# Three more waits ahead of the gathers in the attention walks of a graph network with experts

## The chip, the cores and the metric

The kernel runs on one core of a Trainium2 chip. The metric is the device time of one execution in microseconds (us), as the median of several runs; lower is better. TensorE's clock has two levels, 1.2 and 2.4 GHz; a granted clock of 1.00 in the profile is all of a stretch at the upper one.

## The reference

Four layers, each a graph attention followed by a mixture of experts, over 3125 nodes with 256 features and 50000 edges sorted by destination. What matters here is the attention of layers 0 and 1 and the two attentions of layer 2, which all have this form:

```python
h = jnp.einsum('nd,dhf->nhf', x, W)
al_s = jnp.sum(h * a_src, axis=-1)
al_d = jnp.sum(h * a_dst, axis=-1)
logits = jax.nn.leaky_relu(al_s[src] + al_d[dst], NEG_SLOPE)
m = jax.ops.segment_max(logits, dst, num_segments=num_nodes)
e = jnp.exp(logits - m[dst])
z = jax.ops.segment_sum(e, dst, num_segments=num_nodes)
alpha = e / (z[dst] + 1e-16)
msg = h[src] * alpha[..., None]
out = jax.ops.segment_sum(msg, dst, num_segments=num_nodes)
```

Layer 3's attention also needs a product of the 256 attributes of every edge with a matrix. Its terms are computed in pieces inside the four walks below.

## The kernel before, in words

The function `gat_edges` (from L708) walks over the edges once. It runs four times: for layer 0 and layer 1 (names `l_edges_...`, called from `gat_layer`) and twice for layer 2 (`l2a_edges_...` and `l2b_edges_...`, called from `gat_pair`). The edges are laid out in 416 tiles of 128; 16 tiles are a chunk (CK = 16), so a walk has NCK = 26 chunks. A chunk is worked on in four groups of 4 tiles (GR = 4, NG4 = 4).

Every engine has its own program, written by hand, and they meet by semaphores:

- GpSimd (POOL) issues one gather for each tile (L774): 128 rows of `h_rows`, picked by the tile's source nodes, come from HBM into `stage`. `stage` has SL = 3 slots, one chunk in each. The gathers of group g of chunk c wait until the messages of group g of chunk c - 3 are made (`msg_built`), for then that part of the slot is free. The first three chunks wait for nothing. The order is plain: chunk by chunk, group by group.
- VectorE, in chunk c, makes the messages of a group (`weigh`, L893), rescales the accumulator (L901), makes the logits of chunk c + 1 (`logits`, L828, L831, L833; L831 is the reader of `stage` that waits for the gathers of chunk c + 1), and then takes a step of the running maximum of chunk c + 1 in each group: `tile_ends` (two scans, L838 and L840, and L844), `tile_tops` (scans L853 and L855, L858, L860) and `edge_maxima` (L869, scans L872 and L877, L875). Behind them stand `exponents` (L886, L887) and `nodes_hot` of chunk c + 2 (L823, a transposed one-hot of 2048 columns). In between it adds the finished sums of the group before to the accumulator (L912).
- TensorE (PE), in chunk c, adds up messages by destination (`scatter`, L1081), a group at a time. After group 0 it transposes the logits of chunk c + 1 (L1053, `lg_turned`), after group 1 it places the tile ends (L1057, `ends_placed`), after group 2 the carried maxima (L1062, `inits_made`), in the middle of group 3 it places the rescaling (L1071) and turns the maxima of the edges (L1067, `max_turned`). Around these stand the transposes and products of the edge attributes (L1032, L1039) and the expansion of the destinations' terms of chunk c + 2 (L1047).
- ScalarE (ACT) makes the one-hot matrices for the scatter (L959, L962), the exponentials (L971, L975), and copies the attributes' products out of PSUM (L979, L985).
- SyncE (SP) loads `rel_b` and the edge attributes `ea` and stores the products `e_s` to `e_rows`; it waits for `hotT_built`, `ea_turned` and `e_kept`.

The steps that meet the change, in the words of the code (VectorE, then TensorE):

```python
dve.wait_ge(ends_placed, c + 1)      # tile_tops, before L853
dve.wait_ge(inits_made, c + 1)       # edge_maxima, before L869
dve.wait_ge(max_turned, c + 1)       # exponents, before L886 / L887
...
scatter(c, 1); place_ends(c + 1); attr_terms(c, 0)
scatter(c, 2); place_tops(c + 1); turn_attr(c, m, 1, None)
scatter(c, 3, 0, GR // 2); place_f(c + 1); turn_maxima(c + 1)
```

Of the kernel before, what the change touches and what calls it, by code (L numbers as in the profile page):

```python
# [707 lines left out]
def gat_edges(nc, K, name, h_rows, adp, acc, loops, part):  # L708
# [5 lines left out]
    SL, PER = 3, 6  # L714
    assert (NCK - 2) % PER == 0 and PER % SL == 0 and PER % 2 == 0
    with Phase(nc, name) as ph:
# [49 lines left out]
        with nc.Block() as block:  # L766
            @block.gpsimd
            def _(pool):
                for c in range(NCK):
                    for g in range(NG4):  # L770
                        if c >= SL:
                            pool.wait_ge(msg_built, NG4 * (c - SL) + g + 1)
                        for u in range(g * GR, (g + 1) * GR):
                            nc.gpsimd.indirect_dma_start(out=stage[:, c % SL, u, :], out_offset=None, in_=h_rows,  # L774
                                                         in_offset=bass.IndirectOffsetOnAxis(ap=K.src_t[:, c * CK + u:c * CK + u + 1], axis=0)).then_inc(gathered[c % SL], 16)
# [2477 lines left out]
```

## Time and profile before

| | us |
|---|---|
| median of 3 runs | 7633.64 |
| lowest and highest of them | 7617.78, 7638.52 |
| span of the profiled execution | 7653.2 |
| PE busy | 4967.7 (65%) |
| VectorE busy | 3878.6 (51%) |
| ScalarE busy | 2369.9 (31%) |
| GpSimd busy | 2994.7 (39%) |
| gathers L774 in the four walks | 1664 |

The profiled execution's own time is its span, 7653.2 us, 0.26% above the median of the runs. Busy time of an engine counts its instructions that compute, and for GpSimd the issuing of gathers. Over a program with many stages the shares are averages; what a stage is worth is read in the stretch where it runs.

### The profile page before, as it was taken

What the parts mean: (1) busy time and instruction counts of PE and PEld (TensorE: products, weight loads), DVE (VectorE), ACT (ScalarE), POOL (GpSimd) and SP (SyncE); (2) the same over time, 40 slices, a digit from 0 to 9 for tenths busy, and PEclk for the clock granted to TensorE, in tenths of its full rate; (3) what the DMA queues carried; (4) which work ended last, traced back from release to release, by engine and by line L of the source; (5) the groups of instructions that cost most, each with busy time, mean ns of one, the idle gap of its engine ahead of it and who ended that gap; (6) DMA issues with size and microseconds to landing.
All of it is one profiled execution on the core that took longest, in us unless ns stands there. A gap on an engine that the chain in (4) does not pass through costs nothing. (4 is left out here: it accounts for less than half of the span.)

```text
span 7653.2 us, 80105 instructions
## 1 busy us (share of the span) xinstructions
PE 4967.7 (65%) x19379; PEld 3450.2 (45%) x19380; DVE 3878.6 (51%) x8350; ACT 2369.9 (31%) x5733; POOL 2994.7 (39%) x2942
## 2 busy tenths in 40 slices
PE   1466657726666746666366564777799755557999
PEld 1344435524444534444244443444377533346676
DVE  4355562345556335555355565666611587777211
ACT  0233322213333223333133332444422122245333
POOL 1554423344453034443444434555400277633000
PEclk9677768857777877778677776888899866678899
DMA  4444413334443023333343331111100499954000
GB/s 111 126 129 122 120 40 117 99 97 118 119 123 91 13 78 118 117 120 99 109 122 118 117 101 26 28 26 28 16 17 13 174 374 366 337 155 148 9 12 21
DMA packets 563283, 817.74 MB, mean 107 GB/s; under 512 B 108537, under 2 KB 441942, under 8 KB 562790
## 3 DMA queue, kind: packets, MB, share of 16 engines
q0 software_dynamic: 141088, 377.21, 17.8%
q1 hardware_dynamic: 397914, 425.15, 17.2%
q10 hardware_dynamic: 23952, 11.93, 0.6%
q8 instruction: 93, 1.52, 0.1%
q14 instruction: 236, 1.93, 0.1%
HBM read 656.93 MB, written 157.49 MB: 106 GB/s over the span
## 5 line engine op out<-in xcount | busy, mean ns | idle before, releaser
L774 POOL DMA_INDIRECT l_edges_stage<-l_h_rows,src_t x832 | 801.9, 964 | 861.4 <-DVE l_edges_msg L893 524.2
L1081 PE MATMUL l_edges_ps_sum<-l_edges_msg,l_edges_hot 128*128 128x264 f32 x1664 | 611.2, 512 | 350.7 <-DVE l_attn_acc L912 154.6
L2511 POOL DMA_INDIRECT l_edge_kv<-l_kv_rows,src_t x416 | 471.3, 1133 | 695.7 <-POOLq L2419 547.8
L2933 POOL DMA_INDIRECT l_gate_edges_srow<-l_gate_src_rows,l_gate_edges_idx x512 | 488.7, 954 | 399.5 <-DVE l_gate_edges_val L2990 187.3
L1081 PEld LDWEIGHTS l_edges_ps_sum<-l_edges_msg,l_edges_hot 128*128 128x128 f32 x1664 | 364.4, 244 | 520.4 <-issue 252.1
L3069 PE MATMUL l_gate_edges_ps<-l_gate_edges_wide,l_gate_edges_hot_lo 128*128 128x500 f32 x1024 | 510.0, 657 | 122.5 <-ACT l_gate_edges_hot_lo L3026 94.3
L774 POOL DMA_INDIRECT l2a_edges_stage<-l2a_h_rows,src_t x416 | 399.9, 961 | 450.0 <-DVE l2a_edges_msg L893 280.1
L774 POOL DMA_INDIRECT l2b_edges_stage<-l2b_h_rows,src_t x416 | 399.9, 961 | 433.6 <-DVE l2b_edges_msg L893 269.2
L2564 PE MATMUL l_edge_ps_q<-l_q_q,l_edge_hot 128*128 x832 | 340.7, 581 | 309.4 <-issue 231.8
L1081 PE MATMUL l2b_edges_ps_sum<-l2b_edges_msg,l2b_edges_hot 128*128 128x272 f32 x832 | 318.7, 530 | 181.1 <-issue 80.0
L2564 PEld LDWEIGHTS l_edge_ps_q<-l_q_q,l_edge_hot 128*128 128x128 f32 x832 | 232.7, 293 | 417.5 <-issue 371.5
L1081 PE MATMUL l2a_edges_ps_sum<-l2a_edges_msg,l2a_edges_hot 128*128 128x272 f32 x832 | 308.9, 516 | 154.7 <-issue 86.6
L912 DVE TENSOR_TENSOR l_attn_acc<-l_attn_acc,l_edges_ps_sum 128x264 f32 x832 | 350.2, 421 | 82.4 <-DVE l_attn_acc L912 32.7
L3069 PEld LDWEIGHTS l_gate_edges_ps<-l_gate_edges_wide,l_gate_edges_hot_lo 128*128 128x128 f32 x1024 | 215.9, 217 | 377.2 <-issue 232.7
L2692 DVE SCALAR_TENSOR_TENSOR x<-l_experts_psb,l3f_g,x 128x256 f32<-128x256 f32 x200 | 96.8, 484 | 434.1 <-PE l_experts_psb L2723 434.1
L1081 PEld LDWEIGHTS l2b_edges_ps_sum<-l2b_edges_msg,l2b_edges_hot 128*128 128x128 f32 x832 | 186.7, 250 | 273.1 <-issue 137.3
L2995 DVE TENSOR_TENSOR l_gate_edges_wide<-l_gate_edges_hot_hi,l_gate_edges_val 128x500 f32<-128x500 f32 x512 | 305.5, 669 | 2.2
L2761 ACT ACTIVATE l_experts_hT<-l_experts_psa,l_experts_sc_pair 128x320 f32<-128x320 f32 x320 | 195.3, 611 | 355.1 <-PE l_experts_psa L2714 334.6
L3024 ACT ACTIVATE l_gate_edges_hot_lo<-col,l_gate_edges_nlo 128x128 f32<-128x128 f32 x512 | 156.5, 388 | 436.3 <-DMA l_route_b<-in_L_ffn_gate_b 214.8
L1081 PEld LDWEIGHTS l2a_edges_ps_sum<-l2a_edges_msg,l2a_edges_hot 128*128 128x128 f32 x832 | 181.5, 243 | 242.1 <-issue 146.6
L893 DVE TENSOR_TENSOR l_edges_msg<-l_edges_stage,l_edges_ps_p 128x1056 f32<-128x1056 f32 x208 | 259.5, 1248 | 21.0 <-issue 20.8
L985 ACT COPY l_edges_e_s<-l_edges_ps_e 128x512 f32<-128x512 f32 x96 | 56.3, 586 | 687.7 <-DMA sched_kx<-ends 226.6
(799 smaller groups left out, 11098.5 us busy)
## 6 DMA issues: line engine op xcount, KB each, us to landing
l_edge_e<-e_rows SPq DMA_DIRECT2D x416, 128.0 KB
l_val_rows<-l_edge_vj SPq DMA_DIRECT2D x104, 512.0 KB
l_agg_stage<-l_val_rows SPq DMA_DIRECT2D x52, 1024.0 KB, 5.6
l_edges_rel_b<-rel_rows SPq DMA_DIRECT2D x52, 512.0 KB
l_edges_ea<-in_edge_attr SPq DMA_DIRECT2D x48, 512.0 KB
e_rows<-l_edges_e_s SPq DMA_DIRECT2D x48, 512.0 KB, 5.3
l_experts_w<-in_L_ffn_w SPq DMA_DIRECT2D x32, 512.0 KB, 5.1
l_gate_edges_lo_b<-l_gate_edges_lo_rows SPq DMA_DIRECT2D x64, 256.0 KB
```

The lines of the kernel that those rows point to most:

```text
L774: nc.gpsimd.indirect_dma_start(out=stage[:, c % SL, u, :], out_offset=None, in_=h_rows, in_offset=bass.IndirectOffsetOnAxis(ap=K.src_t[:, ...
L893: nc.vector.tensor_tensor(msg[:, g % 2, :, 0:HW].rearrange("p u (h c) -> p u h c", c=HC), stage[:, i % SL, g * GR:(g + 1) * GR, 0:HW].rear ...
L912: nc.vector.tensor_tensor(to, to, ps_sum[u][:], ALU.add).then_inc(added, 1)
L1081: nc.tensor.matmul(ps_sum[u][:], hot[:, g, u, :], msg[:, g % 2, u, :], start=True, stop=True).then_inc(summed, 1)
L2511: nc.gpsimd.indirect_dma_start(out=kv[:, m, u, :], out_offset=None, in_=kv_rows, in_offset=bass.IndirectOffsetOnAxis(ap=K.src_t[:, n * EB ...
L2564: last = nc.tensor.matmul(ps_q[2 * s + u // 2][:, u % 2, :], hot[:, s, u * P:(u + 1) * P], q[:, bass.ds(ids[n % 4 * EB + u], 1), :].rearra ...
L2692: nc.vector.scalar_tensor_tensor(acc[:, tile, :], psb[(v * GT + t) % 2][:], gates[:, tile, bass.ds(j * 2 + v // NG, 1)], acc[:, tile, :], ...
L2761: nc.scalar.activation(hT[l][:, v % 2, f, half * HALF:half * HALF + cols], psa[n % NA][:, 0:cols], ACT.Relu, bias=sc_pair[:, 1, l, v // NG ...
L2933: nc.gpsimd.indirect_dma_start(out=srow[:, n % 4, u, :], out_offset=None, in_=src_rows, in_offset=bass.IndirectOffsetOnAxis(ap=idx[:, n * ...
L2995: nc.vector.tensor_tensor(wide[:, s, u], bcast(hot_hi[:, n % 3, u, :], GV), val[s][:, u, :].unsqueeze(1).to_broadcast([P, NT, GV]), ALU.mu ...
L3024: nc.scalar.activation(hot_lo[:, s, u, :], K.col[:], ACT.Abs, bias=nlo[:, n * GB + u:n * GB + u + 1]).then_inc(near_lo, 1)
L3069: nc.tensor.matmul(flat, hot_lo[:, n % 2, u, :], wide[:, n % 2, u].rearrange("p t f -> p (t f)"), start=False, stop=False).then_inc(summed, 1)
```

## The change

When gathers of chunk c have to wait at all (c >= 3), group 1 now also waits until TensorE has placed the tile ends of chunk c - 2, group 2 until it has placed the carried maxima of chunk c - 2, and group 3 until it has turned the maxima of chunk c - 2. Group 0 is as before. The program of no other engine is altered.

```diff
                     for g in range(NG4):
                         if c >= SL:
                             pool.wait_ge(msg_built, NG4 * (c - SL) + g + 1)
+                            if g == 1:
+                                pool.wait_ge(ends_placed, c - SL + 2)
+                            elif g == 2:
+                                pool.wait_ge(inits_made, c - SL + 2)
+                            elif g == 3:
+                                pool.wait_ge(max_turned, c - SL + 2)
                         for u in range(g * GR, (g + 1) * GR):
```

## Rows read from the trace of the kernel before

**Rows 1.** The page of the profiled execution, first line.
```profile
span 7653.2 us, 80105 instructions
```

**Rows 2.** Stretches: us; PE, PEld, VectorE, ScalarE, POOL busy (count); clock; DMA share; GB/s.
```profile
300.60:981.20 680.60, 428.78 (x1805) 294.32 (x1802) 360.76 (x838) 226.75 (x572) 339.21 (x352) 0.78 0.42 122
1737.70:2424.40 686.70, 433.04 (x1819) 295.69 (x1815) 361.17 (x838) 227.10 (x573) 339.16 (x352) 0.77 0.43 121
2891.20:3592.50 701.30, 438.89 (x1809) 297.30 (x1806) 367.57 (x860) 238.39 (x661) 338.39 (x352) 0.77 0.41 119
3820.80:4523.00 702.20, 437.71 (x1822) 298.10 (x1821) 367.19 (x859) 238.71 (x661) 338.01 (x352) 0.77 0.42 119
3592.50:3628.60 36.10, 27.27 (x138) 17.05 (x134) 32.23 (x78) 22.00 (x63) 0.00 (x0) 1.00 0.09 30
```

**Rows 3.** Waits of VectorE over the span: us in total, times, longest.
```profile
DVE l_edges_init L869 <- remote: 266.4, 32, 11.6
DVE l2a_edges_init L869 <- DMA l_experts_xs<-pair_rows: 164.3, 20, 11.2
DVE l2b_edges_init L869 <- DMA l_edges_stage<-l_h_rows,src_t: 150.1, 19, 9.1
```

**Rows 4.** A chunk of walk l2a in time: start, us, engine, line [idle before <-releaser].
```profile
3105.62 0.16 DVE L869 COPY l2a_edges_init<-l2a_edges_ps_w 128x2 f32<-128x2 f32 x1 [8.35 <-DMA l_experts_xs<-pair_rows]
...
3110.03 0.29 DVE L886 TENSOR_TENSOR l2a_edges_last_max<-l2a_edges_ps_w,last_t 128x128 f32<-128x128 f32 x1 [1.55 <-PE l2a_edges_ps_w L1067]
...
3114.91 0.96 POOL L774 DMA_INDIRECT l2a_edges_stage<-l2a_h_rows,src_t  x1 [12.09 <-DVE l2a_edges_msg L893]
...
3120.52 0.23 PE L1057 MATMUL l2a_edges_ps_w<-l2a_edges_placed,of_head 128*8 128x32 f32 x2
...
3125.69 0.27 DVE L853 TENSOR_TENSOR_SCAN l2a_edges_run<-links_f,l2a_edges_top,l2a_edges_ps_w 8x32 f32<-8x32 f32 x1 [4.72 <-DMA out_rows<-l_experts_y]
...
3130.80 0.93 PE L1062 MATMUL l2a_edges_ps_w<-ones,l2a_edges_spread 8*128 8x1 f32 x4
...
3134.00 0.96 POOL L774 DMA_INDIRECT l2a_edges_stage<-l2a_h_rows,src_t  x1 [0.30 <-issue]
3137.64 0.59 ACT L985 COPY l2a_edges_e_s<-l2a_edges_ps_e 128x512 f32<-128x512 f32 x1 [12.57 <-DMA pair_rows<-l0f_acc,l0f_slot]
3137.79 0.16 DVE L869 COPY l2a_edges_init<-l2a_edges_ps_w 128x2 f32<-128x2 f32 x1 [7.66 <-DMA l_experts_xs<-pair_rows]
```

**Rows 5.** Another chunk of the same walk in order of time.
```profile
2986.78 0.95 POOL L774 DMA_INDIRECT l2a_edges_stage<-l2a_h_rows,src_t  x1 [3.61 <-DVE l2a_edges_msg L893]
...
2991.03 0.27 PE L1053 MATMUL l2a_edges_ps_w<-ident,l2a_edges_lg 128*128 128x128 f32 x1
...
2995.46 0.42 DVE L838 TENSOR_TENSOR_SCAN l2a_edges_local<-cuts_f,l2a_edges_ps_w 128x128 f32<-128x128 f32 x1 [3.52 <-DMA l_experts_w<-in_L_ffn_w]
...
3000.19 0.28 PE L1057 MATMUL l2a_edges_ps_w<-l2a_edges_placed,of_head 128*8 128x32 f32 x2
...
3000.61 0.27 DVE L853 TENSOR_TENSOR_SCAN l2a_edges_run<-links_f,l2a_edges_top,l2a_edges_ps_w 8x32 f32<-8x32 f32 x1 [1.42 <-PE l2a_edges_ps_w L1057]
...
3005.83 0.16 DVE L869 COPY l2a_edges_init<-l2a_edges_ps_w 128x2 f32<-128x2 f32 x1 [0.77 <-PE l2a_edges_ps_w L1062]
...
3008.28 0.33 PE L1067 MATMUL l2a_edges_ps_w<-ident,l2a_edges_seg_max 128*128 128x128 f32 x1
...
3008.91 0.95 POOL L774 DMA_INDIRECT l2a_edges_stage<-l2a_h_rows,src_t  x1 [0.30 <-issue]
...
3011.05 0.29 DVE L886 TENSOR_TENSOR l2a_edges_last_max<-l2a_edges_ps_w,last_t 128x128 f32<-128x128 f32 x1 [2.36 <-DMA l0f_gb<-in_L_ffn_beta]
...
3015.93 0.95 POOL L774 DMA_INDIRECT l2a_edges_stage<-l2a_h_rows,src_t  x1 [6.07 <-DVE l2a_edges_msg L893]
```

**Rows 6.** Line L774: durations in ns, and who waited for it.
```profile
L774 POOL DMA_INDIRECT l2b_edges_stage<-l2b_h_rows,src_t x416: 948/957/1374, 3722.2 to 4511.8; - x139
...
  DVE l_edges_z L831: 4.4, 2
```

## The prediction, made before the changed kernel was run

> **What bounds the kernel now.** I read the page first, then the stretches of the four attention walks, then the waits, then two single chunks in order of time. The profiled execution spans 7653.2 us [rows 1]. Each walk has 26 chunks. In chunks 1 to 22 the gathers of chunks 4 to 25 are issued beside the arithmetic, and the four stretches that hold them are 680.6, 686.7, 701.3 and 702.2 us long, 352 gathers in each [rows 2]. That is 2770.8 us for 88 chunks, 31.5 us a chunk, 36% of the span. Two chunks at the end of a walk, when no gather is left, take 36.1 us together, so 18.1 us each, with the same arithmetic and the clock granted at 1.00 in place of 0.77 [rows 2]. No engine is full: in the third stretch PE is busy 438.9 of 701.3 us, POOL 338.4 [rows 2]. So a chunk loses 13.4 us to something that the gathers bring.
>
> What it is shows where VectorE waits. Its copy of the carried maxima (L869) alone waits 266.4, 164.3 and 150.1 us [rows 3], 580.8 us in all, and the releasers named there ("remote", a DMA of another phase, the gathers) are not what L869 waits for: in the code it waits for inits_made, which TensorE raises at L1062. In one chunk in order of time [rows 4], the first of 16 gathers starts at 3114.91 and the last at 3134.00, 1.27 us apart. The tile ends (L1057) start on PE at 3120.52 and take 0.2 us, yet VectorE's scan behind them starts at 3125.69. The carried maxima (L1062) start at 3130.80 and take 0.93 us; VectorE's copy starts at 3137.79, 6 us after they end, and ScalarE, idle 12.6 us for a signal of PE, starts at 3137.64. Both start 3.6 us after the last gather started. My reading is that TensorE's signals are held back while a long burst of gathers is under way, and let go together when it has ended. I see no other limit in this stage.
>
> **What the change does, step by step.** Per walk, for chunks 3 to 25 (23 of them), POOL gets three more waits, 276 in all; no instruction that computes and no DMA is added or removed. Group 0 of chunk c still follows the messages of chunk c-3. Group 1 now also waits for ends_placed of chunk c-2, group 2 for inits_made, group 3 for max_turned: each is a signal that TensorE raises about one quarter of a chunk later than the message that released the group so far. So one burst of 16 becomes four bursts, each cut off until the signal that VectorE wants next has got through. Call the starts of the four bursts T0 to T3.
>
> *T0 to T1.* With 4 gathers behind a clear pause, the ends' matmul ends 5.8 us after the first gather (3114.91 to 3120.72 [rows 4]); that is the low end. The other chunk [rows 5] has four bursts of 4 already, by chance: there T0 is 2986.78, and the turned logits, ready on PE at 2991.30, reach the scan L838 at 2995.46, because group 1 had followed group 0 at once and kept the hold up. The last gather of group 0 starts at 2990.7 (2986.78 and three steps of 1.3), and behind the last gather of group 3 the hold is let go after 2.1 us (3008.91 to 3011.05), so 2992.9 would have been possible, 2.5 us sooner. The ends are done at 3000.47, 13.7 us after T0, less 2.5 is 11.2; the high end. I take 10.0, near the high end, since group 3 of the chunk before will stand right ahead of group 0, as a burst of 8, and the logits will be held much as in rows 5.
>
> *T1 to T2.* From the scan L853 at 3000.61 to the copy L869 at 3005.83: 5.2 us, with gathers running [rows 5]. Above it a full hold: 3.8 us to the last of four gathers and 3.6 us more as in rows 4, 7.4. I take 5.6.
>
> *T2 to T3.* 3005.83 to 3011.05 is 5.2 us with gathers, L1067 ending at 3008.61 and held until 2.1 us after the gather at 3008.91 [rows 5]; without gathers 4.4 (3105.62 to 3110.03 [rows 4]); above, 7.4 again. I take 5.2.
>
> *T3 to the next T0.* 4.9 us in either chunk (3110.03 to 3114.91 [rows 4], 3011.05 to 3015.93 [rows 5]). POOL itself needs four times 1.27, 5.1, before it can start group 0, so this part becomes POOL's. Group 3 now also meets VectorE's building of the transposed one-hot (L823, after L887), which few gathers do today. Rows bound that: a gather takes 957 ns in the middle and 1374 at most [rows 6], so between nothing and 0.4 us. I take 5.4. The Trainium skill, SBUF — State Buffer, section "Who interferes with whom", says that a tensor_scalar in a two-port mode holds GpSimd off the shared port until it is done; by that rule alone the loss could be the whole length of L823; no gather of this trace was lengthened by more than 0.4 us.
>
> Sum: 10.0 + 5.6 + 5.2 + 5.4 = 26.2; I add 0.5 for chunks that are longer than the pattern for reasons I can't place, 26.7. The ends give 5.8 + 5.2 + 4.4 + 5.1 = 20.5 and 11.2 + 3 x 7.4 = 33.4. Present pattern as a check: 3105.62 to 3137.79 is 32.2 us [rows 4]. The gain is 31.5 - 26.7 = 4.8 us a chunk, 88 times, 422 us. I cost nothing for chunk 0 of each walk, where 48 gathers run ahead without a wait, and for the last three chunks, which have none. I cost nothing for the later landing of the gathers: group 3 goes off at most a chunk later and is wanted two chunks on by L831, which today waited on gathers 4.4 us in the first two walks together [rows 6]; if that cover went, L831 would wait and every chunk with it. Behind POOL's new waits stand only further gathers; SP's queue and the phase's end wait for none of them. 7653.2 - 422 = 7231 for the profiled execution; the median of the runs, 7633.64, lies 20 us under its span, so 7211, and I say 7210.
>
> **The rivals.** *Signals pass freely* (13%). If a burst of 4 holds nothing, and 8 in a row little, a chunk is 20.5 to 24.5 us, gain 7 to 11 us, 616 to 968 in all: 6665 to 7020. For: the copy L869 waited 0.77 us there, against 7.66 in rows 4 [rows 5]. Against: L1067 in the same rows, ready at 3008.61 and seen at 3011.05.
>
> *The spacing takes most of it back* (17%). The chunk of rows 5 was split in four by chance and still took 29.2 us (3015.93 - 2986.78). If only the last tenths change there, 29 to 31.2 us: 7415 to 7610.
>
> *Slower* (12%). If a burst of 4 is already long enough to hold every signal for the full 3.6 us behind its last gather, each stage is 7.4 us, and stage T0 has a second round trip in it, as logits and ends follow each other (2995.46 to 3000.19, 4.7 us [rows 5]): 4 x 7.4 + 4.7 = 34.3, 2.8 us a chunk over today, 247 us: up to 7880. POOL would idle while PE's signals wait, and the overlap of gathers with the stage behind would be lost. It decides from a mean hold that brings the sum over 31.5. Against it stand the 2.1 us behind the last gather and the short wait of L869 in rows 5.
>
> *No change* (6%). The hold may have nothing to do with the bursts' length: 7634. The Trainium skill, SBUF — State Buffer, section "Who interferes with whom", has it that a DMA never contends with a compute engine and that PE and ACT wait for nobody; by that rule the gathers could not cost TensorE's readers anything. Rows 2 (18.1 us against 31.5) speak against it, though the clock differs as well and might be cause rather than effect: were PE at 0.77 the cause, the chunk's idle would be PE's busy time and not waits of 6 us.
>
> **How the numbers follow.** The forecast, 24.5 to 29 us a chunk, 7020 to 7415, has 52%. A measurement of this kernel can tell about 0.3%, 23 us. Faster by more: 52 + 13 + 17 = 82%; within 6%; slower 12%. Range: up to 7640, which takes in no change and leaves the slower case out, and down to 6900, leaving some 5% below.
>
> **What would show it.** Right: POOL's gathers (L774) wait for PE's L1057, L1062 and L1067; bursts of 4, 4 and 8; L869's wait falls from 580.8 us to under 150; the four stretches shrink to about 590 us each; granted clock there above 0.77. T0 wrong: L838 waits about as long as L853 does today, or not at all. Wrong as a whole: L853, L869 and L886 each wait 2 us or more after PE has ended, in every chunk, and the distance of L893's first groups stays at 31 us or grows.

## The result, and the profile after

The changed kernel takes 7437.02 us as the median of 4 runs (7404.3 to 7447.07), the kernel before, beside it, 7636.08 us (7617.78 to 7644.19): a ratio of 0.974, with a 95% interval of 0.9711 to 0.977. The profiled execution spans 7445.3 us, 208 less than before [rows 1].

The four stretches of chunks 1 to 22, cut by the same instructions as before [rows 2], with the same columns:

```profile
299.50:955.10 655.60, 460.62 (x1805) 318.51 (x1805) 362.50 (x837) 227.39 (x573) 338.85 (x352) 0.79 0.42 127
1710.40:2361.40 651.00, 448.61 (x1806) 311.50 (x1805) 362.68 (x837) 228.37 (x574) 337.37 (x352) 0.80 0.43 128
2826.20:3442.40 616.20, 445.78 (x1804) 298.12 (x1804) 367.10 (x860) 239.48 (x657) 342.97 (x352) 0.81 0.46 135
3669.10:4292.80 623.70, 447.94 (x1805) 301.81 (x1804) 367.40 (x860) 240.79 (x660) 341.09 (x351) 0.80 0.45 133
```

They sum to 2546.5 us against 2770.8: 224.3 us less, 28.94 us a chunk against 31.49. The start of each walk, from its first gather to the first message of chunk 1, is 2.3 to 3.8 us shorter, 13.3 us in all; its end, from the first message of chunk 23 on, is 0.9 to 3.6 us longer, 7.7 us in all. The rest of the program gives about 22 us back, most of it behind the last message of the last walk, 3099.9 us against 3081.1. The kernels below, with the same program there and on chips where the kernel before takes about 7640 us, have 3067.6 to 3109.9 us in that place, so I read this as scatter.

The waits of POOL and of VectorE over the span (us in total, times, longest). The line numbers are 6 higher than before: L844 is the first reader of the turned logits, L859 of the tile ends, L875 of the carried maxima (L869 of [rows 3]), L893 of the turned maxima, L834 of the expansion of the destinations' terms.

```profile
POOL l_edges_stage L780 <- PE l_edges_ps_w L1063: 331.7, 41, 15.0
DVE l_edges_x L893 <- remote: 205.0, 45, 7.3
DVE l_edges_ad L834 <- remote: 170.8, 39, 23.3
DVE l_edges_local L844 <- remote: 104.5, 30, 5.0
DVE l_edges_init L875 <- remote: 22.5, 4, 9.9
DVE l_edges_init L875 <- PE l_edges_ps_w L1068: 21.5, 38, 1.3
```

The wait for the carried maxima, 580.8 us by the rows shown before [rows 3] and 613.0 us with the smaller ones of the same line, is 102 us now with all of them (44.0 here for layers 0 and 1). In its place stand waits for the turned maxima (L893), the turned logits (L844) and the expansion (L834). One chunk of layer 0, in order of time:

```profile
565.10 1.04 POOL L780 DMA_INDIRECT l_edges_stage<-l_h_rows,src_t  x1 [2.56 <-remote]
...
570.22 0.97 POOL L780 DMA_INDIRECT l_edges_stage<-l_h_rows,src_t  x1 [0.31 <-issue]
...
572.70 0.42 PE L1059 MATMUL l_edges_ps_w<-ident,l_edges_lg 128*128 128x128 f32 x1
...
574.03 0.97 POOL L780 DMA_INDIRECT l_edges_stage<-l_h_rows,src_t  x1 [0.30 <-issue]
...
576.76 0.42 DVE L844 TENSOR_TENSOR_SCAN l_edges_local<-cuts_f,l_edges_ps_w 128x128 f32<-128x128 f32 x1 [4.90 <-remote]
...
581.37 0.28 PE L1063 MATMUL l_edges_ps_w<-l_edges_placed,of_head 128*8 128x32 f32 x2
...
582.43 0.95 POOL L780 DMA_INDIRECT l_edges_stage<-l_h_rows,src_t  x1 [7.43 <-PE l_edges_ps_w L1063]
...
585.55 0.60 PE L1068 MATMUL l_edges_ps_w<-ones,l_edges_spread 8*128 8x1 f32 x4
...
586.19 0.16 DVE L875 COPY l_edges_init<-l_edges_ps_w 128x2 f32<-128x2 f32 x1
...
587.47 0.96 POOL L780 DMA_INDIRECT l_edges_stage<-l_h_rows,src_t  x1 [0.30 <-issue]
...
588.61 0.33 PE L1073 MATMUL l_edges_ps_w<-ident,l_edges_seg_max 128*128 128x128 f32 x1
...
591.25 0.96 POOL L780 DMA_INDIRECT l_edges_stage<-l_h_rows,src_t  x1 [0.30 <-issue]
...
594.01 0.29 DVE L893 TENSOR_TENSOR l_edges_x<-l_edges_lg,l_edges_ps_w 128x128 f32<-128x128 f32 x1 [5.00 <-remote]
...
594.76 1.04 POOL L780 DMA_INDIRECT l_edges_stage<-l_h_rows,src_t  x1 [2.55 <-remote]
```

The gathers go in two bursts of eight. The first is group 3 of one chunk (from 565.10) and group 0 of the next (from 570.22, T0), the second is group 1 (582.43, T1) and group 2 (587.47, T2). Group 2 starts 5.04 us after group 1, four gathers' pitch: its new wait ends before POOL gets there. A signal raised early in a burst passes: the carried maxima, placed at 585.55 with 0.60 us of matmuls, are read at 586.19, 3.8 us into the burst. A signal raised later does not: the turned logits are done at 573.12 and read at 576.76, 2.7 us after the last gather of the burst has started (574.03); the turned maxima are done at 588.94 and read at 594.01, 2.8 us after the last gather (591.25). So the chunk is 12.2 + 5.0 + 7.3 + 5.1 = 29.6 us.

It isn't the reader that is slow. The trace also records the semaphores' updates: that of the turned logits at 576.62, 3.5 us after their matmul's end and 0.14 before the scan, that of the turned maxima at 593.99, 5.05 us after theirs and 0.02 before L893. The one of the tile ends, outside a burst, comes 0.01 us after its matmul (581.65, 581.66). As the profile models the ends of matmuls, this doesn't say whether in a burst the matmul itself or only its update is late.

The means from the starts of the gathers' groups, chunks 4 to 25 of each walk, whose gathers go beside chunks 1 to 22 (worked out from all rows of L780, us):

| | T0 to T1 | T1 to T2 | T2 to T3 | T3 to T0 | a chunk, 1 to 22 |
|---|---|---|---|---|---|
| layer 0 | 12.28 | 5.25 | 6.88 | 5.40 | 29.80 |
| layer 1 | 11.80 | 5.08 | 7.19 | 5.53 | 29.59 |
| layer 2, first | 10.42 | 5.52 | 6.45 | 5.62 | 28.01 |
| layer 2, second | 10.94 | 5.51 | 6.43 | 5.55 | 28.35 |
| all | 11.36 | 5.34 | 6.74 | 5.53 | 28.94 |

Chunk 3, the first whose gathers wait, is left out: its T0 to T1 is 18.6 to 20.6 us.

In layer 2 chunks of 24 to 26 us and of 31 to 36 us alternate over parts of the walks: T0 to T1 is about 7.8 us in the short ones and 13.7 to 16.7 in the long ones, 14 of the 44. One of the long ones, in order of time:

```profile
3089.77 0.95 POOL L780 DMA_INDIRECT l2a_edges_stage<-l2a_h_rows,src_t  x1 [1.79 <-DMA l_experts_xs<-pair_rows]
...
3092.86 0.29 DVE L892 TENSOR_TENSOR l2a_edges_last_max<-l2a_edges_ps_w,last_t 128x128 f32<-128x128 f32 x1 [0.97 <-PE l2a_edges_ps_w L1073]
...
3103.94 0.95 POOL L780 DMA_INDIRECT l2a_edges_stage<-l2a_h_rows,src_t  x1 [0.30 <-issue]
...
3107.08 0.56 DVE L834 TENSOR_REDUCE l2a_edges_ad<-l2a_edges_ps_ad 128x128 f32<-128x384 f32 x1 [9.22 <-remote]
...
3115.15 0.95 POOL L780 DMA_INDIRECT l2a_edges_stage<-l2a_h_rows,src_t  x1 [10.26 <-PE l2a_edges_ps_w L1063]
```

Here group 2's wait did last (1.79 us idle before 3089.77). The turned maxima then passed, 3.1 us into the burst (3092.86), and groups 3 and 0 followed with no pause: a burst of 12, up to 3103.94. It held the expansion until 3107.08, 3.1 us after its last gather, the logits stand behind that, and T1 is 3115.15, 15 us after T0 (3100.17).

### The profile page after: what moved, and what is told of

Read it like the earlier page. It is cut to its first block and busy times, and to the rows that moved or that the text cites. A ratio compares the mean times of both kernels' runs of the same rounds, so it can differ in the third digit from the quotient of the medians.

```text
span 7445.3 us, 80381 instructions
## 1 busy us (share of the span) xinstructions
PE 5031.1 (68%) x19379; PEld 3497.1 (47%) x19380; DVE 3881.1 (52%) x8350; ACT 2376.9 (32%) x5733; POOL 3003.7 (40%) x2942
## 5 line engine op out<-in xcount | busy, mean ns | idle before, releaser
L780 POOL DMA_INDIRECT l_edges_stage<-l_h_rows,src_t x832 | 799.6, 961 | 806.6 <-PE l_edges_ps_w L1063 331.7
L780 POOL DMA_INDIRECT l2a_edges_stage<-l2a_h_rows,src_t x416 | 404.7, 973 | 361.8 <-issue 111.7
L780 POOL DMA_INDIRECT l2b_edges_stage<-l2b_h_rows,src_t x416 | 403.8, 971 | 362.3 <-issue 113.3
L1045 PE MATMUL l_edges_ps_e<-l_edges_we,l_edges_eaT 128*128 128x256 f32 x768 | 238.9, 464 | 86.0 <-issue 73.5
```

The costliest lines, as they stand in the source:

```text
L1045: last = nc.tensor.matmul(ps_e[0:n, u * D:(u + 1) * D], eaT[:, u, k, 0:n], we[:, k, :], start=(k == 0), stop=(k == DC - 1))
```

## The experiments

The first kernels take single waits of the change away.

**One wait, on the ends.** Edit against the changed kernel:

```diff
                             if g == 1:
                                 pool.wait_ge(ends_placed, c - SL + 2)
-                            elif g == 2:
-                                pool.wait_ge(inits_made, c - SL + 2)
-                            elif g == 3:
-                                pool.wait_ge(max_turned, c - SL + 2)
```

> Of the three new waits only the one of group 1 (ends_placed) is kept. Theory (TensorE's signals are held while gathers follow one another and are let go 2.6 us after the last one has started; the first 4 us of a burst let them pass): groups 1 to 3 go as one burst of 12 from T1, the turned maxima come free at T1 + 13.9 + 2.6 = 16.5, group 0 starts 4.6 later, alone behind a pause, so that ends_placed is there 6 to 7.8 us after it. 27.1 to 28.9 us a chunk, against 28.9 with all three waits: 7360 to 7440 us. Rival (each wait brings its share of the gain): a third of the 199 us of the change, about 7570.

Measured: 7358.04 us against 7644.86 of the kernel before beside it, 0.963 (0.9614 to 0.9646), 28.20 us a chunk. One chunk in order of time:

```profile
445.91 0.96 POOL L776 DMA_INDIRECT l_edges_stage<-l_h_rows,src_t  x1 [3.60 <-DVE l_edges_msg L895]
...
459.37 0.29 DVE L889 TENSOR_TENSOR l_edges_x<-l_edges_lg,l_edges_ps_w 128x128 f32<-128x128 f32 x1 [6.77 <-remote]
459.81 1.34 POOL L776 DMA_INDIRECT l_edges_stage<-l_h_rows,src_t  x1 [0.30 <-issue]
465.54 0.95 POOL L776 DMA_INDIRECT l_edges_stage<-l_h_rows,src_t  x1 [4.39 <-DVE l_edges_msg L895]
```

Groups 1 to 3 are a burst of 12 (445.91 to 459.81), which holds the turned maxima for 6.8 us and lets them go 0.4 us before its last gather starts, not after it; group 0 then stands alone, since its messages are late, and T0 to T1 is 8.5 us, the last stage 8.9 to 9.5 in most chunks. One wait alone brings at least as much as the three. The chunk lies where it was expected, but by parts that make up for each other: the turned maxima are free 13.5 us after T1 in place of 16.5, group 0 starts 6.2 us later in place of 4.6, and T0 to T1 takes 8.5 in place of 6 to 7.8.

**Without the wait of group 2, and with that of group 3 alone.**

```diff
-                            elif g == 2:
-                                pool.wait_ge(inits_made, c - SL + 2)
```

```diff
-                            if g == 1:
-                                pool.wait_ge(ends_placed, c - SL + 2)
-                            elif g == 2:
-                                pool.wait_ge(inits_made, c - SL + 2)
-                            elif g == 3:
+                            if g == 3:
                                 pool.wait_ge(max_turned, c - SL + 2)
```

> The wait of group 2 (inits_made) is left out, those of groups 1 and 3 stay. Theory: group 2 starts 5.0 us after group 1 in most chunks of the changed kernel, which is POOL's own pace, so this wait decides nothing: within 25 us of the changed kernel's 7437. Rival (the three waits together make four bursts): loses a part of the gain, 7500 or more.

> Of the three new waits only the one of group 3 (max_turned) is kept. Theory: groups 3, 0 and 1 go as a burst of 12, the turned logits of the next chunk are held until 16.5 us after it began, then ends, carried maxima and turned maxima follow, each 4 to 6 us later: about 31 us a chunk, as without any wait, 7560 to 7680 us. Rival (each wait brings its share): about 7570; rival (it is the wait ahead of the loads that matters, since gathers no longer meet them): near the changed kernel, 7440.

Measured beside the same kernel before: 7304.23 us, 0.9557 (0.954 to 0.9574), 27.60 us a chunk; and 7467.66 us, 0.976 (0.9738 to 0.9783), 29.74 a chunk. Both came out faster than expected, by 108 us and 92 us against the near ends, and no theory or rival named the first. The second lies 31 us above the changed kernel, so near the rival by which it is the wait of group 3 that matters. Its bursts aren't the one of 12 that was expected: group 1 starts 7.6 us after group 0 in the mean, so groups 3 and 0 are a burst of eight, and groups 1 and 2 another in most chunks. What is held most there is the expansion:

```profile
DVE l_edges_ad L830 <- remote: 347.7, 44, 28.6
```

The stretches of layer 2 without the wait of group 2:

```profile
2792.60:3365.40 572.80, 440.12 (x1805) 295.80 (x1804) 366.58 (x859) 240.74 (x662) 344.17 (x352) 0.84 0.50 145
3591.90:4169.40 577.50, 437.85 (x1805) 294.84 (x1804) 366.46 (x859) 240.60 (x661) 344.17 (x352) 0.84 0.50 144
```

Layer 2 gains most (616.2 to 572.8, 623.7 to 577.5), where short and long chunks alternated; T0 to T1 falls there from 10.4 and 10.9 us to 8.1 and 8.3. In the changed kernel group 2's wait lasts 0.8 or 1.5 us in 18 of the 44 chunks of layer 2, mostly with what follows as in the chunk at 3089.77 above. A short pause in one place took away a longer one in a better place. Each pause stands or falls with the others, so the waits don't add.

**A quarter of the bytes.** Against the kernel before; each gather brings a quarter of a row, `stage` holds ones elsewhere, so the messages aren't the reference's.

```diff
+                narrow = h_rows.rearrange("n (a b) -> (n a) b", a=4)
-    nc.gpsimd.indirect_dma_start(out=stage[:, c % SL, u, :], ..., in_=h_rows,
+    nc.gpsimd.indirect_dma_start(out=stage[:, c % SL, u, 0:RW // 4], ..., in_=narrow,
```

> The kernel before, with each gathered row cut to a quarter (68 of 272 numbers, 272 bytes for 1088); the number of gathers, their rows and their order stay. It leaves out three quarters of each row (the slot is filled with ones once), so messages and logits are not the reference's. Theory that the hold comes from the gathers' count and their pace on GpSimd: a chunk stays at 30 to 32 us, 7550 to 7700 us. Rival that it comes from the bytes moved (DMA engines or HBM busy): the hold goes with three quarters of the bytes, a chunk falls to POOL's 20.3 us or a little over, 6650 to 6900 us.

Measured: 7674.72 us, 1.0042 (1.0023 to 1.006), 31.40 us a chunk. The first stretch (DMA share 0.27 and 68 GB/s against 0.42 and 122 [rows 2]), the gathers' queue in it (packets, MB, share of the DMA engines), and a wait of VectorE, L873 being the reader of the carried maxima:

```profile
307.20:993.40 686.20, 428.10 (x1786) 290.43 (x1787) 360.56 (x837) 225.40 (x569) 338.16 (x352) 0.77 0.27 68
```

```profile
q0 software_dynamic: 11264, 12.28, 12.5%
```

```profile
DVE l_edges_init L873 <- remote: 249.2, 29, 11.1
```

The hold doesn't come from the bytes or from busy DMA engines. The number of gathers and the scattered rows are as before.

**A chip without the hold.** The next six runs were on another chip, where the kernel before takes 6333.78 and 6330.87 us. Five kernels were tried there, one of them twice, with edits that all stand below: plain DMAs in place of the gathers (whole tiles, and halves), four waits, three waits for logits, ends and turned maxima, and a pause.

> The kernel before, with each gather replaced by a plain DMA of 128 consecutive rows (the same bytes, the same slots, the same waits, issued by GpSimd too). It leaves the indices out, so messages are those of other rows. Theory that it is GpSimd's issuing of DMAs one after another, whatever their kind, that holds TensorE's signals: 7500 us or more, L869 still waits 500 us or more. Rival that it is the indirect form alone: the hold is gone, 18 to 22 us a chunk, 6500 to 6850 us.

> The changed kernel with a fourth wait: group 0 also waits until the logits of chunk c - 2 are turned (lg_turned). Theory: what was mis-sized is the stretch T0 to T1 (12.2 us in most chunks of the changed kernel), because group 0 follows group 3 at once and the burst of 8 holds the turned logits for 11.5 us. With the wait, group 3 stands alone, the logits pass, groups 0 and 1 go as one burst and hold the carried maxima until T0 + 11.5, group 2 follows, the turned maxima pass 4.4 us into it, and the next logits are held until 11.5 us after group 2: 23 to 24.5 us a chunk, against 28.9 and 27.6 without the wait of group 2: 6930 to 7080 us. Rival (POOL is already short of time and every wait more only idles it): 7437 or slower.

> As the run with four waits, but without the one of group 2 (carried maxima), so waits on lg_turned, ends_placed and max_turned. Theory: groups 0, 1 and 2 go as one burst of 12, and the carried maxima, ready 7.8 us into it, are held in it: 26 to 28 us a chunk, 7150 to 7350 us, slower than with the wait, though the same wait cost 133 us when group 0 had none. Rival (the wait of group 2 always costs, as between the changed kernel and the run without it): faster than the run with four waits.

> The kernel without the wait of group 2, and behind the first gather of group 3 a small memset that the second one waits for, so that the burst of groups 3 and 0 is some 0.4 us longer. Theory (in the third and fourth walk a gather lengthened from 0.95 to 1.34 us does the same by chance, and the turned logits slip through): the stretch from group 0 to group 1 falls from 12.1 to about 8 us in the first two walks, up to 180 us less than without the pause where the kernel before takes 7640: 7180 to 7280 us. Rival (it is the additional work of the third and fourth walk that makes the difference, not the gap): no change, 7300 to 7370 us. Where the kernel before takes 6334: within 1% of it.

> Waits on lg_turned for group 0, ends_placed for group 1, max_turned for group 3, none for group 2. Where the kernel before takes about 7640: groups 0, 1 and 2 go as one burst of 12 and hold the carried maxima, 27 to 29 us a chunk, 7270 to 7420 us, slower than the 7247 with all four waits. Rival (the wait of group 2 is never worth its place): 7100 to 7240 us.

> Plain DMAs in place of the gathers, each split into two of 64 partitions, so 32 a chunk at about 0.53 us each: 17 us of issuing a chunk, near the 20.2 of the gathers. It leaves the indices out, so messages are those of other rows. Theory that the indirect form brings the hold: none here, 18 to 20 us a chunk, 6200 to 6500 us, L869 waits under 60 us in all. Rival that any long run of DMAs from GpSimd brings it: 25 us a chunk and more, 7000 us or more, where the kernel before takes about 7640.

Measured there, in this order: 6148.26 us, 0.9703 (0.9688 to 0.9718); 6335.57, 1.0006 (0.9997 to 1.0015); 6339.03, 1.0008 (0.9999 to 1.0017); 6347.61, 1.003 (1.0017 to 1.0043); 6329.76, 0.9998 (0.9988 to 1.0008); 6263.43, 0.9891 (0.9875 to 0.9908). The first stretch of the kernel with four waits, and its wait for the carried maxima in layers 0 and 1:

```profile
262.20:709.80 447.60, 367.46 (x1806) 246.47 (x1805) 359.26 (x837) 226.84 (x572) 340.67 (x351) 0.94 0.61 186
```

```profile
DVE l_edges_init L877 <- PE l_edges_ps_w L1070: 1.8, 2, 0.9
```

A chunk is 20.56 us, near POOL's own 16 x 1.26 = 20.2, TensorE's signals are seen at once, and waits change nothing, as there is nothing to save. The changed kernel itself wasn't run there. These runs don't tell the theories apart, but they show that the loss which the gathers bring isn't there on every chip. The kernels were run again where the kernel before takes about 7650 us.

**The changed kernel again, four waits, and without group 2's.** The first and the last are the kernel as changed, and the one without group 2's wait as above. Four waits, against the changed kernel:

```diff
                             pool.wait_ge(msg_built, NG4 * (c - SL) + g + 1)
-                            if g == 1:
+                            if g == 0:
+                                pool.wait_ge(lg_turned, c - SL + 2)
+                            elif g == 1:
                                 pool.wait_ge(ends_placed, c - SL + 2)
```

> The changed kernel once more, on whatever chip comes, since the last three runs were on a chip where the kernel before took 6334 us and not 7640. Theory (the change lives on the hold of TensorE's signals alone): where the kernel before takes about 7640, 7437; where it takes about 6334 (chunks of 20.4 us, POOL's own pace, no hold), ratio 0.998 to 1.003. Rival (the waits cost something wherever there is no hold): 1 to 5% slower on such a chip.

> The kernel with a wait for each of the four groups (lg_turned, ends_placed, inits_made, max_turned) again. Where the kernel before takes about 7640: 23 to 24.5 us a chunk, 6930 to 7080 us, as expected before. Rival: the additional wait only idles POOL, 7437 or slower. Where the kernel before takes about 6334: ratio 0.998 to 1.003, as measured.

> The kernel without the wait of group 2 again. Where the kernel before takes about 7640: 7304, so 133 us faster than the changed kernel beside it on the same chip. Where it takes about 6334: no difference, 0.998 to 1.003, since no signal is held and POOL's pace of 1.26 us a gather sets the chunk.

Measured against 7646.92 us of the kernel before: the changed kernel 7408.0, 0.9683 (0.9634 to 0.9731), 28.80 us a chunk, so its gain is there on a second chip; four waits 7247.12, 0.9481 (0.9449 to 0.9513), 26.97 a chunk; without group 2's wait 7365.89, 0.9623 (0.9585 to 0.9661), 28.36. The last lies 42 us under the changed kernel beside it, and the two intervals overlap: what leaving out group 2's wait is worth (133 us across chips, 42 here) isn't settled.

Four waits gain 160 us more than three, in the stage that they were meant for: T0 to T1 falls to 5.6 us. But the chunk is 27 us and not 23 to 24.5, and the kernel takes 7247 us and not 6930 to 7080, since the time shows up at two other signals:

```profile
DVE l_edges_ad L836 <- remote: 216.9, 48, 23.2
DVE l_edges_init L877 <- remote: 136.3, 46, 9.2
```

```profile
579.97 0.95 POOL L782 DMA_INDIRECT l_edges_stage<-l_h_rows,src_t  x1 [2.00 <-remote]
...
588.98 0.96 POOL L782 DMA_INDIRECT l_edges_stage<-l_h_rows,src_t  x1 [0.30 <-issue]
...
591.62 0.56 DVE L836 TENSOR_REDUCE l_edges_ad<-l_edges_ps_ad 128x128 f32<-128x384 f32 x1 [0.53 <-remote]
...
594.96 0.96 POOL L782 DMA_INDIRECT l_edges_stage<-l_h_rows,src_t  x1 [5.02 <-PE l_edges_ps_w L1061]
```

Groups 2 and 3 are one burst here (579.97 to 588.98). It holds the expansion, read 2.64 us after its last gather, and group 0 waits for logits which stand behind the expansion: T3 to T0 is 9.2 us in the mean in place of 5.5, T1 to T2 7.0.

This kernel also answers a doubt of the prediction, whether the clock could be cause rather than effect. The stretch of layer 0 is 90 us shorter than before, at the same granted clock (0.78 here and in [rows 2]), so these 90 us are not the clock's:

```profile
291.80:882.30 590.50, 438.67 (x1806) 307.94 (x1805) 361.90 (x838) 228.74 (x572) 339.64 (x352) 0.78 0.46 141
```

**Plain DMAs in place of gathers.** Against the kernel before; consecutive rows are read, the indices are left out, so the output isn't the reference's. The second form has 32 DMAs of 64 rows a chunk, to keep POOL as busy as the gathers did; the reader of `stage` waits for twice the count.

```diff
-    nc.gpsimd.indirect_dma_start(out=stage[:, c % SL, u, :], ...)
+    nc.gpsimd.dma_start(stage[:, c % SL, u, :], h_rows[u * P:(u + 1) * P, :])
```

```diff
+    for k in range(2):
+        half = slice(k * P // 2, (k + 1) * P // 2)
+        nc.gpsimd.dma_start(stage[half, c % SL, u, :], h_rows[u * P + k * P // 2:u * P + (k + 1) * P // 2, :])
```

> Plain DMAs of 128 consecutive rows in place of the gathers again; the indices are left out, so messages are those of other rows. Where the kernel before takes about 7640: if GpSimd's issuing one DMA after another holds the signals whatever their kind, 7400 us or more; if it is the gathers' indirect form, or their issuing for 0.95 us each, chunks of 18 to 22 us and 6150 to 6850 us. Where the kernel before takes about 6334: 6148, ratio 0.970, as measured.

> As for the same kernel before, 17 us of plain DMAs a chunk, indices left out: where the kernel before takes about 7640, 6200 to 6600 us if only the indirect form brings the hold, 7000 or more if any long run of DMAs does; where it takes about 6331, 0.989 as measured.

Measured: 6387.65 us against 7646.92, 0.8353 (0.8324 to 0.8382), 19.60 us a chunk; and 6470.25 against 7649.07, 0.846 (0.8442 to 0.8478), 20.29 a chunk. The issuing instructions of the first (durations in ns, lowest, median, highest):

```profile
L774 POOL DMA_DIRECT2D l_edges_stage<-l_h_rows x832: 536/538/938, 200.0 to 1790.6; - x167
```

A stretch of the second, and its wait for the carried maxima:

```profile
283.00:700.00 417.00, 346.40 (x1722) 233.88 (x1721) 342.47 (x798) 216.12 (x547) 351.86 (x675) 0.94 0.68 193
```

```profile
DVE l_edges_init L870 <- PE l_edges_ps_w L1063: 3.1, 3, 1.3
```

POOL is busy 351.9 of 417 us with an unbroken run of DMAs, as many bytes are moved, at 193 GB/s, and nothing is held. So what holds TensorE's signals is neither a busy POOL nor the bytes, but something that comes with the gathers' indirect form. Three things changed together here and aren't told apart: the indirect form, the time of issuing one (0.95 us against 0.54), and the rows, which are scattered in the gathers and the same 2048 consecutive ones in every chunk of the plain DMAs. Gathers with consecutive indices weren't run.

**A pause inside the burst.** Against the kernel without group 2's wait: after the first gather of group 3 POOL writes a small tile and waits for it.

```diff
+                            if c >= SL and u == 3 * GR:
+                                nc.gpsimd.memset(idle[:], 0.0).then_inc(idled, 1)
+                                pool.wait_ge(idled, c - SL + 1)
```

> As for the same kernel before: where the kernel before takes about 7640, 7180 to 7280 us if the gap lets the turned logits slip through (the stretch from group 0 to group 1 falls from 12.1 to about 8 us in the first two walks), 7300 to 7370 if not; where it takes about 6331, ratio 1.003 as measured.

Measured: 7136.7 us (7122.09 to 7160.99) against 7649.07, 0.9327 (0.93 to 0.9354), 26.01 us a chunk. It is the fastest version that computes the reference, 300 us under the changed kernel (on another chip) and 512 under the kernel before on its own, and 43 us below the range that was expected. A stretch of layer 0 and one of layer 2, then a typical chunk:

```profile
293.80:862.50 568.70, 437.06 (x1806) 295.96 (x1805) 360.52 (x838) 227.66 (x573) 343.03 (x375) 0.84 0.50 146
...
2644.80:3222.70 577.90, 437.24 (x1805) 294.24 (x1804) 367.26 (x860) 240.97 (x663) 348.56 (x375) 0.83 0.50 144
```

```profile
550.49 1.04 POOL L780 DMA_INDIRECT l_edges_stage<-l_h_rows,src_t  x1 [2.40 <-remote]
...
551.53 0.19 POOL L783 MEMSET l_edges_idle<- 128x96 f32 x1
551.99 0.96 POOL L780 DMA_INDIRECT l_edges_stage<-l_h_rows,src_t  x1 [0.27 <-POOL l_edges_idle L783]
...
557.96 0.27 PE L1062 MATMUL l_edges_ps_w<-ident,l_edges_lg 128*128 128x128 f32 x1
...
558.39 0.42 DVE L847 TENSOR_TENSOR_SCAN l_edges_local<-cuts_f,l_edges_ps_w 128x128 f32<-128x128 f32 x1 [1.53 <-PE l_edges_ps_w L1062]
...
562.94 0.95 POOL L780 DMA_INDIRECT l_edges_stage<-l_h_rows,src_t  x1 [2.43 <-PE l_edges_ps_w L1066]
```

The second gather starts 1.50 us after the first, where it was 1.34 in the changed kernel. The logits are done at 558.23 and read at 558.39, 7.9 us into a burst of eight, while in the changed kernel those done 8.0 us into such a burst (573.12) waited until 576.76. T0 to T1 is 7.1 to 7.7 us in most chunks in place of 12.2, and a chunk of layers 0 and 1 takes 25.8 us in place of 29.0 to 29.6 without the pause (two chips). So a step of 0.2 us, with the small write in it, is worth more than 3 us. Why so little is enough isn't shown. A hint is that layer 2 had its gap already: there the first gather of group 3 takes 1.34 us and the next starts 1.64 us after it (2944.56 and 2946.20 in the kernel without group 2's wait), most of its chunks had a T0 to T1 below 9 us without the pause, and with it a chunk of its two walks takes 26.3 and 26.1 us, where it was 26.0 and 26.3 without on one chip and 27.5 and 26.9 on another. But some chunks of layer 2 with that gap are long all the same. What is left is the hold of the turned maxima (T2 to T3 7.2 us; 211.8 us in 48 waits at L896 in layers 0 and 1).

**Waits for logits, ends and turned maxima** (four waits without that of group 2):

```diff
+                            if g == 0:
+                                pool.wait_ge(lg_turned, c - SL + 2)
+                            elif g == 1:
                                 pool.wait_ge(ends_placed, c - SL + 2)
-                            elif g == 2:
-                                pool.wait_ge(inits_made, c - SL + 2)
```

> As for the same kernel before: where the kernel before takes about 7640, 7270 to 7420 us if groups 0, 1 and 2 in one burst hold the carried maxima, 7100 to 7240 if the wait of group 2 isn't worth its place; where it takes about 6331, no difference as measured.

Measured: 7458.27 us, 0.9748 (0.973 to 0.9766), 29.66 us a chunk; it misses, and is 211 us over the four waits (on another chip, with the same time before). With group 0 cut off, the carried maxima fall late in a burst and are held:

```profile
DVE l_edges_init L875 <- remote: 338.8, 47, 9.6
```

So group 2's wait is worth nothing, or costs, while group 0 runs on, and is worth having once group 0 waits.

## Why the prediction was right and wrong

**The mechanism was right.** Signals of TensorE are held while gathers run, and more gaps between gathers let them through. The copy of the carried maxima waits 102 us in place of 613 (under 150 was named), the granted clock is 0.79 to 0.81 in the stretches (above 0.77), POOL waits for TensorE's steps, and the time fell, inside the range. The experiments narrow it down: the bytes and a busy POOL don't matter, and with plain DMAs the hold is gone. What the prediction said of its end, that all is let go when the burst has ended, isn't exact: signals also pass early in a burst, and some are let go inside it.

**The size was not.** 426 us were forecast and 199 came; the stretches are 616 to 656 us and not about 590. Two terms of the sum were too small, T2 to T3 by 1.54 us a chunk and T0 to T1 by 1.36. By its own steps:

- *T0 to T1*, taken as 10.0 (between 5.8 and 11.2): measured 11.36 in the mean and 12.2 in the typical chunk of layers 0 and 1, beyond the high end. The place was right, a burst of eight that holds the logits. Their release, put 6.1 us after T0 in the high end, comes 6.5 after it (576.76 - 570.22); then follow 4.9 to the end of the tile ends' matmul (581.65), where rows 5 had 5.0; and POOL starts 0.8 us after that (582.43), which the sum had left out altogether. On top of that I took 10.0 under the 11.2 of the row, with no row for the difference. This is one of the two steps that failed.
- *T1 to T2*, 5.6: measured 5.34, POOL's own pitch in most chunks.
- *T2 to T3*, 5.2: measured 6.74, and 7.3 in the typical chunk, close to the full hold of 7.4 that stood as the upper end. (That 7.4 was 3.8 us to the last gather and 3.6 behind it; what came is 3.8, 2.8 and another 0.75 until POOL starts, so it hit partly by luck.) The step took over a chunk [rows 5] in which the signal came late against the burst; here group 2 follows group 1 with no gap, and the prediction's bursts of 4, 4 and 8 are two of 8. The step failed to ask of each new wait whether it lasts at all: the carried maxima pass 3.8 us into the burst, before POOL has issued group 1. This is the other step that failed.
- *T3 to T0*, 5.4: measured 5.53. The first gather of group 3 meets the building of the one-hot (L829) as was foreseen: 1.04 us in layer 0 (565.10), against 0.95 to 0.97 of the others, 1.34 in layer 2. So 0.1 to 0.4 us, within the bounds, and no more than the stretch in which the two overlap: in the kernel without group 2's wait the one-hot ran from 2944.32 for 0.75 us, the gather from 2944.56 for 1.34. The Trainium skill (SBUF — State Buffer, "Who interferes with whom") lets a two-port tensor_scalar hold GpSimd off until it is done, and this agrees with it.
- *The surcharge of 0.5* for odd chunks: they exist (T0 to T1 of 13.7 to 16.7), and are contained in the means above.

The chunk is 28.94 and not 26.7: 2.24 us, 88 times, 197 us short. The start of the walks, costed at nothing, gave 13.3; the last chunks, costed at nothing too, took 7.7; the gathers' later landing costs nothing that shows (L837, the former L831, waits 2.1 us for gathers in the four walks).

**The rivals.** *Spacing takes most of it back* had 17% and 7415 to 7610 us: the time, 7437, falls into it, and the chunk, 28.94, at its lower edge of 29. It should have had the larger share, as its witness was the one chunk of the trace that was already split in four [rows 5] and took 29.2 us, which is almost what came. *Signals pass freely* was wrong wherever the kernel before takes about 7640, and is what plain DMAs show: 19.6 to 20.3 us a chunk, where the rival had 20.5 to 24.5. *Slower* had two stages right for the typical chunk of layers 0 and 1: T0 to T1 at full hold with a second round trip, 7.4 + 4.7 = 12.1 (12.2 came), and T2 to T3 at 7.4 (7.3). Its other two, 7.4 each, came at 5.0 and 5.1, POOL's own pitch. *No change* is out, by 199 us; so is the rule named beside it (the Trainium skill, SBUF — State Buffer, "Who interferes with whom"), that DMA never contends with a compute engine, as far as it was read to cover signals: L844 and L893 wait for matmuls that the profile has as finished. It speaks of memory ports, and as a rule on those nothing here speaks against it: a quarter of the bytes changed nothing.

## What to carry to other kernels

When a reader starts microseconds after its producer has ended, and the releaser that the trace names has nothing to do with it, look at what else was being issued, and measure the distance from the last of that to the start: here it is nearly the same for bursts of the same length, 2.7 and 2.8 us behind eight gathers in the chunk above. It isn't one number: it was 2.1 us behind four [rows 5], 3.1 behind twelve (3103.94 to 3107.08) and 3.6 behind sixteen [rows 4]. A wait that is to space out work must be placed so that it really lasts where the signal wanted next is raised; draw up the bursts that result, with their lengths, before adding up stages, and expect waits not to add. Two waits on data and a short forced pause in the right place (7136.7 us) did more than three waits on data (7408 to 7437) or those two alone (7304 to 7366). And measure on more than one chip: versions that gain 2.5 to 6.7% on the others gained nothing on one.

## What was not expected of the hardware

- The kernel before takes 7636 to 7649 us beside most kernels here and 6331 to 6334 on one chip, twice. About 960 of the 1300 us are the walks' (31.49 us a chunk, and 20.56 with four waits there). What differs about that chip stays open.
- A burst of gathers lets signals pass in about its first 4 us (3.1 and 3.8 us into it in the chunks above), then holds most of them. Those that it holds to the end are seen 2.1 us after the start of its last gather in a burst of four, 2.6 to 2.8 in one of eight, 3.1 in one of twelve and 3.6 in one of sixteen; others are let go inside it, as the turned maxima 13.5 us into a burst of twelve (445.91 to 459.37). What in the chip does this is not shown; only that bytes, plain DMAs and a busy POOL are not it.
- An indirect gather of 128 rows takes POOL 0.95 us at a pitch of 1.26, a plain DMA of 128 rows 0.54.
